# Layer 1 hands its node blocks on earlier: a two-layer graph network on one Trainium2 core

## The reference: what is computed

```python
def reference(x, src, dst, edge_type_16, ...):
    # relational layer
    W = einsum('rb,bio->rio', w_comp, weight);  h = einsum('ni,rio->rno', x, W)
    x = layernorm(x + segment_sum(h[etypes, src], dst) + h_bias)
    # mean layer
    agg = segment_sum(x[src], dst) / max(degree, 1)
    return layernorm(x + (x @ W_self + b_self) + agg @ W_neigh)
```

## Time and profile before

| | us |
|---|---|
| median of 3 runs (4057.68 to 4067.66) | 4063.3 |
| the profiled execution's own time | 4019.25 |
| its span | 4015.4 |
| mean granted TensorE clock | 0.668 |

### The profile page before, as it was taken

One profiled execution on the slowest core, in us unless ns is written; L12 is line 12 of the kernel. 1 busy time (PEld: TensorE's weight loads), 2 busy tenths in 40 slices (PEclk: granted clock), 3 DMA queues, 4 the chain that ended last, 5 costly groups with the idle time before them and its releaser, 6 DMA issues.

```text
span 4015.4 us, 35728 instructions
## 1 busy us (share of the span) xinstructions
PE 2164.1 (54%) x12534; PEld 2038.8 (51%) x12534; DVE 1388.0 (35%) x3584; ACT 316.5 (8%) x572; POOL 2464.1 (61%) x2604
## 2 busy tenths in 40 slices
PE   2555666656566556655566676613443443434344
PEld 1445565655566556555556666613443343433344
DVE  5233222222223222222222222303455565655434
ACT  1011000000000000000000100100000000000001
POOL 6665556655665566665666666475666666666662
PEclk9767667676767667667776667755556666666666
DMA  4923333333333333333333333221222222222232
GB/s 112 278 61 88 96 91 102 99 97 91 102 99 93 92 100 106 88 97 93 100 98 97 99 102 99 72 63 42 53 55 54 53 60 53 62 54 59 63 82 56
DMA packets 256690, 347.55 MB, mean 87 GB/s; under 512 B 47110, under 2 KB 188431, under 8 KB 256504
## 3 DMA queue, kind: packets, MB, share of 16 engines
q0 software_dynamic: 106448, 266.31, 24.0%
q1 hardware_dynamic: 150056, 78.90, 6.7%
HBM read 314.29 MB, written 43.57 MB: 89 GB/s over the span
## 4 chain that ended last, share of the span: by engine, by line
PE 32%; issue 26%; another core or an unknown queue 24%; DVE 13%; DVEq 1%; ACT 1%; POOL 1%; DMA 0%; SPq 0%; ACTq 0%; POOLq 0%
PE zps L1867 13%; PE yps L1877 5%; PE yps L1892 4%; DVE acc L1727 2%; PE tps L1877 2%; PE zps L1967 2%; DVE acc L1548 2%; DVE acc L1570 2%; DVE acc L1662 1%; DVE acc L1638 1%; PE tps L1858 1%; PE tps L1892 1%; PE zps L1962 1%; DVE acc L1731 1%
## 5 line engine op out<-in xcount | busy, mean ns | idle before, releaser
L1355 POOL DMA_INDIRECT rows<-x_x_rows,src_t x1469 | 1392.5, 948 | 905.8 <-issue 422.0
L1867 PE MATMUL zps<-acc,rows 128*128 128x168 f32 x3328 | 797.4, 400 | 326.8 <-issue 251.9
L1369 POOL DMA_INDIRECT rows<-x_rows,picked_mem x739 | 699.3, 946 | 375.8 <-issue 212.4
L1867 PEld LDWEIGHTS zps<-acc,rows 128*128 128x128 f32 x3328 | 709.9, 261 | 387.8 <-issue 383.8
L1548 DVE TENSOR_TENSOR acc<-oh,tps 128x1344 f32<-128x1344 f32 x208 | 323.3, 1554 | 375.6 <-remote 308.6
L1877 PE MATMUL yps<-oh,rows 128*128 128x21 f32 x1920 | 291.7, 280 | 285.7 <-issue 285.1
L1877 PEld LDWEIGHTS yps<-oh,rows 128*128 128x128 f32 x1920 | 307.0, 230 | 270.6 <-issue 270.1
L1570 DVE TENSOR_TENSOR acc<-acc,yps 128x63 f32 (+1 forms) x544 | 118.8, 218 | 869.5 <-remote 728.8
L1967 PE MATMUL zps<-acc,rows 128*128 128x128 f32 (+1 forms) x1478 | 289.6, 359 | 140.6 <-issue 139.9
L1967 PEld LDWEIGHTS zps<-acc,rows 128*128 128x128 f32 x1478 | 264.8, 267 | 158.5 <-issue 158.0
L1936 PE MATMUL yps<-acc 128*128 128x24 bf16 (+7 forms) x1472 | 92.5, 193 | 434.1 <-issue 335.1
(11 more groups left out here) (253 smaller groups left out, 1829.2 us busy)
## 6 DMA issues: line engine op xcount, KB each, us to landing
rows<-x_x_rows,src_t POOLq DMA_INDIRECT x1469
acc<-in_edge_type_dram SPq DMA_DIRECT2D x207, 64.0 KB
rows<-x_rows,picked_mem POOLq DMA_INDIRECT x739
x_x_rows<-in_x_dram SPq DMA_DIRECT2D x20, 576.0 KB
x_x_rows<-zrow SPq DMA_DIRECT2D x20, 576.0 KB
xin<-in_x_dram SPq DMA_DIRECT2D x24, 256.0 KB
x_rows<-xout SPq DMA_DIRECT2D x24, 256.0 KB
out_dram<-xout SPq DMA_DIRECT2D x24, 256.0 KB
```

Of the source, the lines that this page charges most:

```text
L1355: gather = pool.indirect_dma_start(out=wide_rows[:, g % WIDE_SLOTS, c, :], out_offset=None, in_=table, in_offset=bass.IndirectOffsetOnAxis ...
L1369: pool.indirect_dma_start(out=rows[:, j % SLOTS, c, :], out_offset=None, in_=x1_rows[0:n_nodes, :], in_offset=bass.IndirectOffsetOnAxis(ap ...
L1867: last = nc.tensor.matmul(zwins[g % 2][:, c // HALF, c % HALF // 2], slot_rows(g, c), a[:, g % 4, c], start=(c % 2 == 0), stop=(c % 2 == 1))
```

## The change

`BEHIND` is 6 instead of 7: every step of `front` from the third quad on stands one group sooner, so each reader of x1 comes one group sooner, and the steps for quads 0 and 1 both fall on group 24. With it the late edges shrink from 931 chunks (117 late groups) to 927 (116).

The quad's steps stand sooner: staged in slot 2lp+2 (was 2lp+3), turned at the start of slot 2lp+3 (was the end of 2lp+4), added and normalised in slot 2lp+3 (was 2lp+5), cleared in 2lp+5 (was 2lp+7). On ACT root and normalisation now follow the staging directly, in the same slot.

The last two groups are no longer a pair for the additions: each is projected, counted and added by itself (`finish_group`), with a PSUM bank of its own for the last, and of the last group only its 5 real chunks are summed (was 8). PE's order at the end is written out.

```diff
-BEHIND = 7
+BEHIND = 6
...
-            staged_at = {2 * last_pair(k) + 3: k for k in range(all_quads)}
-            turned_at = {2 * last_pair(k) + 4: k for k in range(all_quads)}
-            out_at = {2 * last_pair(k) + 5: k for k in range(all_quads)}
-            cleared_at = {2 * last_pair(k) + 7: k for k in range(all_quads)}
+            staged_at = {2 * last_pair(k) + 2: k for k in range(all_quads)}
+            turned_at = {2 * last_pair(k) + 3: k for k in range(all_quads)}
+            out_at = dict(turned_at)
+            cleared_at = {2 * last_pair(k) + 5: k for k in range(all_quads)}
...
                         if g in staged_at:
                             stage_quad(staged_at[g])
-                        if g in out_at:
-                            roots_of(n1, out_at[g])
-                            normalise_quad(n1, out_at[g])
+                            roots_of(n1, staged_at[g])
+                            normalise_quad(n1, staged_at[g])
...
-                        if g % 2 and 3 <= g < groups + 2:
+                        if g % 2 and 3 <= g < groups:
                             add_sums(g - 3)
+                            add_sums(g - 2)
+                        if groups <= g < groups + 2:
                             add_sums(g - 2)
...
+                    def finish_group(g):
+
+                        duos = duos_of(g)
+                        pe.wait_ge(counted, pairs)
+                        nc.tensor.matmul(windows_of(g)[:, 2, 0:duos], ones_b[:, :], counts_b[:, (pairs - 1) % 2, g % 2, 0:duos],
+                                         start=True, stop=True)
+                        pe.wait_ge(w1.z_copied, g + 1)
+                        for b in range(n_bases):
+                            last = nc.tensor.matmul(windows_of(g)[:, 1, 0:duos], wb[:, b, :], zsb[:, g % 4, 0:duos, b, :],
+                                                    start=(b == 0), stop=(b == n_bases - 1))
+                        last.then_inc(w1.y_done, 1)
...
-                    for g in range(groups + 6):
+                    for g in range(groups - 2):
                         if g % HALF == 2 and g // HALF + 1 < 2 * bodies:
                             scale_by_relation(g // HALF + 1)
-                        if g < groups:
-                            sum_group(g)
-                        if g % 2 == 0 and 2 <= g <= groups:
-                            project_pair(g // 2 - 1)
-                        if g < groups:
-                            early_sums(g)
-                            if g % 2:
-                                count_pair(g // 2)
                         if g in turned_at:
                             turn_quad(turned_at[g])
+                        sum_group(g)
+                        if g % 2 == 0 and g:
+                            project_pair(g // 2 - 1)
+                        early_sums(g)
+                        if g % 2:
+                            count_pair(g // 2)
                         if g in loops_at:
                             turn_loops(loops_at[g])
+
+                    project_pair(pairs - 2)
+                    sum_group(last_group - 1)
+                    early_sums(last_group - 1)
+                    finish_group(last_group - 1)
+                    turn_quad(last_quad - 1)
+                    sum_group(last_group)
+                    early_sums(last_group)
+                    finish_group(last_group)
+                    turn_quad(last_quad)
```

More of the change, by code:

```diff
@@ L1033, in last_pair @@
                 return (done_at(k) - 1) // 2
-            staged_at = {2 * last_pair(k) + 3: k for k in range(all_quads)}
-            turned_at = {2 * last_pair(k) + 4: k for k in range(all_quads)}
-            out_at = {2 * last_pair(k) + 5: k for k in range(all_quads)}
-            cleared_at = {2 * last_pair(k) + 7: k for k in range(all_quads)}
+            staged_at = {2 * last_pair(k) + 2: k for k in range(all_quads)}
+            turned_at = {2 * last_pair(k) + 3: k for k in range(all_quads)}
+            out_at = dict(turned_at)
+            cleared_at = {2 * last_pair(k) + 5: k for k in range(all_quads)}
+            assert last_pair(last_quad - 1) == pairs - 2
             loops_at = {(1, 3, 7, 9)[k]: k for k in range(len(quads))}
@@ L1046, in gnn_kernel @@
                 for use in (([("pair", g // 2)] if g < groups and g % 2 == 0 else []) + ([("quad", turned_at[g])] if g in turned_at else [])
-                            + ([("loops", loops_at[g])] if g in loops_at else [])):
+                            + ([("loops", loops_at[g])] if g in loops_at else [])
+                            + ([("single", g)] if g == last_group else [])):
                     bank_of[use] = len(users) % len(banks)
@@ L1084, in real_chunks, with duos_of, windows_of, products_before @@
                 return last_group_chunks + 1 if g == last_group else CPG
+            def duos_of(g):
+                return -(-real_chunks(g) // 2)
+            def windows_of(g):
+                return last_windows if g == last_group else windows[g // 2][:, :, g % 2 * DUOS:(g % 2 + 1) * DUOS]
+            def products_before(g):
+                return g // 2 + (2 if g == last_group else 1)
             lead = 5
@@ L1561, in add_sums @@
                         _, starts = nc.values_load_multi_w_load_instructions(
-                            base[0:1, g * DUOS:(g + 1) * DUOS], engines=DVE_ONLY, min_val=0, max_val=n_nodes,
+                            base[0:1, g * DUOS:g * DUOS + duos_of(g)], engines=DVE_ONLY, min_val=0, max_val=n_nodes,
                             skip_runtime_bounds_check_because="clamped to the number of nodes, and acc is padded")
-                        dve.wait_ge(w1.y_done, g // 2 + 1)
+                        dve.wait_ge(w1.y_done, products_before(g))
                         after(dve, w1.group_added, g)
-                        for c in range(DUOS):
+                        for c in range(duos_of(g)):
                             target = kinds3[:, first:3, bass.ds(starts[c], SPAN)]
@@ L1569, in add_sums @@
                                 dve.wait_ge(w1.rmw, g * (DUOS - 1) + c)
-                            add = nc.vector.tensor_tensor(target, target, windows[g // 2][:, first:3, g % 2 * DUOS + c, :],
+                            add = nc.vector.tensor_tensor(target, target, windows_of(g)[:, first:3, c, :],
                                                           ALU.add)
-                            add.then_inc(w1.rmw if c < DUOS - 1 else w1.group_added, 1)
+                            add.then_inc(w1.rmw if c < duos_of(g) - 1 else w1.group_added, 1)
                     def mark_early():
@@ L1865, in sum_group @@
                         rows_arrived(w1, g)
-                        for c in range(CPG):
+                        for c in range(real_chunks(g)):
                             last = nc.tensor.matmul(zwins[g % 2][:, c // HALF, c % HALF // 2], slot_rows(g, c), a[:, g % 4, c],
-                                                    start=(c % 2 == 0), stop=(c % 2 == 1))
+                                                    start=(c % 2 == 0), stop=(c % 2 == 1 or c == real_chunks(g) - 1))
                         last.then_inc(w1.z_done, 1)
@@ L1874, in early_sums @@
                             bank_free("pair", g // 2)
+                        if g == last_group:
+                            bank_free("single", g)
                         if not narrow(g):
-                            for c in range(CPG):
-                                last = nc.tensor.matmul(windows[g // 2][:, 0, g % 2 * DUOS + c // 2],
+                            for c in range(real_chunks(g)):
+                                last = nc.tensor.matmul(windows_of(g)[:, 0, c // 2],
                                                         wide_rows[:, g % WIDE_SLOTS, c, d:2 * d], oh1[:, g % 6, c],
-                                                        start=(c % 2 == 0), stop=(c % 2 == 1))
+                                                        start=(c % 2 == 0), stop=(c % 2 == 1 or c == real_chunks(g) - 1))
                             last.then_inc(rows_read, 1)
```

1 line of the change is left out of this document (added).

## The result

| | before | after |
|---|---|---|
| median of 6 runs each | 4056.84 (4051.81 to 4067.66) | 3934.5 (3922.01 to 3942.71) |
| the profiled execution's own time | 4019.25 | 3933.16 |
| its span | 4015.4 | 3931.5 |
| mean granted TensorE clock | 0.668 | 0.677 |

The change makes the kernel faster: ratio 0.9702 (0.9684 to 0.972), 122 us by the medians. The forecast was 3996, 67 less than the median of 4063.3 then known. The time lies in the range stated, 3930 to 4055, but within 5 us of its lower end and under the likeliest case's own range of 3960 to 4021; it is nearer to the 3926 of the rival by which PE's stop costs nothing.

The account below looks back on a forecast made before the run. The prediction took POOL's waits for the degrees' store, set by PE's written order with no engine full, as the bound: -154.7 + 90 + 3 + 0 - 5.8 = -67 us, from 4063.3 to 3996, range 3930 to 4055.

Parts of the forecast that it names:

- likeliest case: Whole kernel: 3996 us, own range 3960 to 4021, at prices of 2.5 to 5.5 us per quad; chance 0.64.
- PE's stop costs nothing: Rival, PE ahead of the turn: 4.6 us to spare cover its stop, about 1 us per quad, 3926; chance 0.14.
- The removed waits: POOL, groups 32 to 176: what quads 2 to 18 cost above the floor of 11.5 us a group goes, -154.7 us.
- long waits stay: Rival, steps of `front`: stores land late or SP is busy, the nine long waits hardly shrink, 4055; chance 0.10.
- The new price: POOL at group 2lp+7: new waits cost 4.3 us for each of quads 2 to 22, 90 us in all.
- wait for PE's buffers: POOL at group 101 for quad 10: PE's turn delays group 97's sums and early sums, a 2.8 us wait, in every quad.
- wait for the store: POOL at group 101 for quad 10: waits 3.4 us for the degrees' store instead of 16.6 at group 102.
- factor of 1.2: POOL: a wait in the middle of a pair costs 5.3/4.29 = 1.2 of its length, so 3.5 becomes 4.3 us.
- Quads 19 to 22: Late layer 1: these had no wait of their own before, yet are charged 4.3 us each for the new waits.
- PE in the slow stretch: Rival: PE's pushed work falls into the burst of gathers, 9.4 us for each of 21 quads, 4103; chance 0.12.
- The start: Groups 24 and 25: quad 1, now needed at group 24, lands at about 311; +3 us, between -1 and +10.
- Layer 2: Late gathers: four fall away, 927 instead of 931, at 1.44 us each, -5.8 us.

Follow-up runs that it names:

- again: The kernel before with nothing changed, run on a quick chip: 3314.38 us, ratio 1.000.
- t7: The kernel before with only the quad's steps sooner, `BEHIND` still 7 and the old end of layer 1, on a quick chip: 3317.24 us, ratio 1.0008.
- whole: The changed kernel itself, unchanged, on a quick chip: 3306.51 us against 3315.56 for the kernel before, ratio 0.9973.
- lag2: Kernels before and changed, PE's sums of group g held until group g+2's rows arrive, quick chip: 3508.82 and 3402.48 us, 0.9697 against each other.
- whole7: The changed kernel with `BEHIND` 7 instead of 6, on a chip where the kernel before takes 4058.95 us: 3921.7 us, ratio 0.9655.

## Why the prediction was right, and where its terms were off

**What bounds the kernel** held. The long waits were the written order and no full engine: with the order changed, the nine waits (11.8 to 17.0 us) became 4 to 4.6, at the predicted group (101 for quad 10), and groups 32 to 176 took 1714.8 us where 1728 were forecast. What the prediction did not say is that this rests on PE being three groups behind POOL. It read that off the trace as times and took it as given; `again`, `t7` and `whole` show that without it the change gives 0.3%, and the `lag2` pair that it alone brings 3% back.

**The removed waits** (-154.7): the "long waits stay" rival fell, for no wait of 16 us is left in layer 1's steps after group 24. But not all of the 154.7 us were waits at the steps of `front`. The 5.3 us that groups 92 to 100 lose in before were put down to the 4.29 us at group 93; half of them belong to another wait, which the rows shown leave out:

```profile
1231.37 0.94 POOL L1355 DMA_INDIRECT rows<-x_x_rows,src_t  x1 [5.91 <-PE yps L1877]
```

This is group 98. From group 92 to 96 before takes 1205.70 - 1157.12 = 48.6 us, 2.6 above two pairs at the floor; the other 2.7 come with group 98. Between groups 33 and 176 before has 17 such single waits of 4.7 to 7.6 us, and some 40 of the 154.7 us are theirs; after has four, of 6.2 to 8.4. That most of them went was not forecast, and no run shows why they did.

**The new price** (21 x 4.3 = 90) is the term that was mis-sized. The floor in after is 1293.78 - 1270.59 = 23.19 us a pair, so 72 pairs are 1669.7 and 17 quads cost 45.1 us, 2.65 each; with nothing for quads 19 to 22 it is 2.1 for each of 21, under the 2.5 to 5.5 of the likeliest case. That groups 32 to 176 came within 13 us of the forecast is in part luck: the 17 quads cost 28 us less than the 73 reckoned, and the floor, held fixed in the prediction, took 14.4 of them back (72 pairs by 0.20). Three parts of the price were off.

- The wait for PE's buffers was forecast at 2.8 us. The staging was laid behind both additions, from 1257.1 to 1257.7, so that it begins 2.7 us after group 100's start. At quad 10 it runs between them, beginning 1.0 after that start, and the turn took 1.09 us and not 1.5. The wait is there all the same, and shorter: `whole7`, where no store hides it, has 1.97 us at group 101 and 1.9 to 2.1 at every group 2lp+7. In after the wait for the store, which ends later, stands over it at nine quads, as the prediction had it. The "stop costs nothing" rival was wrong on the wait, and near on its price (below).
- The wait for the store was forecast at 3.4 us and is 4.29. The staging began 1.7 us sooner than laid, but from there to POOL's start are 13.0 us and not 10.7: DVE's tables stand between turn and addition (2.2 us), and the landing took 0.4 more. The step moved past work on DVE that the prediction had not counted. For the eight quads with an even step the forecast of no store wait was right, so the sign "3 to 5 us at group 2lp+7 of each quad" came true at nine quads only; the others have 2.0.
- The factor of 1.2 on a wait in the middle of a pair was the misread row above: with group 98's wait taken out, before's 4.29 us cost 2.6 too, a factor of 0.6. After such a wait the next pauses give part of it back. After quad 10's 4.29 us, POOL doesn't pause at group 102, pauses 3.42 us at 103 and only 2.04 at 104, so that the 4.29 us cost 2.6; in the same way 2.0 cost 0.65. Nine times 2.6 and eight times 0.65 are 29 us; the other 16 are mostly the four single waits.

**Quads 19 to 22** were charged 17 us and cost nothing: groups 176 to 206 take 353.6 us against 354.3. Their 2 us waits are there (groups 177, 185, 193, 203), but the single waits in that stretch are longer in before: 5.93 and 6.48 us at groups 182 and 198, where after has 4.17 and 4.23.

**PE in the slow stretch** did not come: the sums of group 97 took 3.35 us, begun at 1224.27, and POOL's waits there stayed below 5 us. PE's stop is 9.8 us long and not about 3; in before PE spent most of that time on group 97's sums, which stood apart from 1246.18 on. The clock was low in that stretch in both kernels, as predicted: 0.50 from 1213 on in after, and from 1244 on in before. It was back at 1.00 from about 1227 on. The Trainium skill (TensorE: Matmul & The Clock Gate, Part 1, on the HAM clock gate) ties the level to the array's recent work. The windows above agree in both directions, 1.00 while PE worked, 0.50 while it stood and 1.00 after it had worked again; and the following group, 98, which by the dearer reading would have stayed low, ran at 1.00.

**The start** was +8.8 and not +3, still within the bound of +10. The store lands for group 24 at 314.2 and not at 311, and from group 25 (324.16, against 318.45) to 32 go another 3.1 us: 83.3 against 80.1. In `whole7`, where quad 1 is needed at group 25 only, that group begins at 318.50 as before, but from there to group 32 are 83.7 us, so these 3 us are not due to `BEHIND` 6.

**The end of layer 1** (0, within 4) was +2.0 us from group 206 to layer 2 here, and -1.6 on the quick chip. **Layer 2** (-5.8) gave 0.6, so by the prediction's own sign this part was wrong: the gathers were 927 as forecast, but each took 1342.3/926 = 1.450 us against 1.444.

**From the profile to the runs** the prediction added -67 to the median. By the profiled executions the change was -84, by the runs -122. In the paces of after (23.19 us a pair, 1.450 us a late gather) before would have been some 24 us longer than its trace shows: 92 pairs by 0.20 and 930 gathers by 0.006. That may account for 24 of the 38 us; there is no second trace of before at that pace, and the rest stays open.

## What to carry to other kernels

A wait on a store that depends on the written order is paid in groups of distance between the engines, so state that distance as a condition of the forecast: where it was one group, the same edit gave 0.3%. Price a wait by what the following waits save, over several of its kind and several pairs, and look in the stretch for other waits before you charge it all to one. When a hand-over is made sooner, try it once without moving the reader sooner too: here the reader's group was worth four gathers and cost nine waits.

## What the runs showed of the hardware

The same kernel took 4057 to 4059 us on two occasions and 3314 to 3316 on two other chips, a gap of 22% that none of the edits comes near. On the slower ones POOL stops 3.3 us after each sixteen gathers, in layer 2 too (in after at 3243.70 and 3266.69, sixteen gathers apart). In after that makes 23.19/16 = 1.449 us a gather in layer 1 and 1.450 in layer 2, although layer 2's rows are half as wide; on a quick chip (`again`) it is 1.25 in both, which is POOL's own 0.95 and the gap of 0.30. So what the slower chips add goes, in these traces, by the gather and not by its bytes. A limit on the gathers' rate would also explain why the pauses shrink after a wait, but no run shows what it is. On the slower chips, besides, PE's products stand apart in a burst of gathers, with nothing named as the reason. The timeline of PE in after, sums of group 103 (start, length):

```profile
1281.47 0.53 PE L1880 MATMUL zps<-acc,rows 128*128 128x168 f32 x2
1283.47 0.45 PE L1880 MATMUL zps<-acc,rows 128*128 128x168 f32 x2 [1.47 <-issue]
1284.19 0.44 PE L1880 MATMUL zps<-acc,rows 128*128 128x168 f32 x1 [0.27 <-issue]
1286.29 0.72 PE L1880 MATMUL zps<-acc,rows 128*128 128x168 f32 x2 [1.66 <-issue]
```

These sums need until 1294.4, over 12 us; in `again` a group's sums near there take 2.5 to 4.8 us in one piece, and PE waits ahead of them for gathered rows. The DMA engines are no busier on the slower chip (share 0.34 against 0.42 in the windows above). What slows gathers and products there was not found. Ratios taken on one chip hold on another only if the waits that they stem from are there.
